# Weighted sums of heads 0 to 7 and 8 to 15 in two banks of PSUM, each half copied by itself

## The chip, the cores and the metric

The kernel runs on one core of a Trainium2 chip. The metric is the time of one execution on the device in microseconds (us). The core has five engines that run their own queues of instructions and wait for one another by semaphores: TensorE (PE in the profile, with its weight loads as PEld), VectorE (DVE), ScalarE (ACT), GpSimd (POOL) and SyncE (SP, which issues DMAs). TensorE writes into PSUM, which has eight banks of 128 x 512 floats; VectorE and ScalarE read it from there.

## The reference

Two transformer blocks in float32 over 16 batches of 128 rows and 128 channels, both with a condition vector per batch. The first has one attention head and an MLP. The second, to which the change belongs, has 16 heads of 8 channels, a padding mask and an MLP:

```python
h = _modulate(_layernorm(x), shift_msa, scale_msa)
qkv = h @ qkv_w.T + qkv_b             # 16 heads of 8 channels
attn = einsum('bhnd,bhmd->bhnm', q, k) * 8 ** -0.5
attn = softmax(where(mask, attn, -1e9))
out = einsum('bhnm,bhmd->bhnd', attn, v)     # the weighted sums
x = x + gate_msa * (out @ proj_w.T + proj_b)
h = _modulate(_layernorm(x), shift_mlp, scale_mlp)
x = x + gate_mlp * (gelu(h @ fc1_w.T + fc1_b) @ fc2_w.T + fc2_b)
```

## The kernel before

Everything stays in the core's memory. Each engine's program is written out by hand, so the order of the instructions in the source is the order on the engine, and `wait_ge` and `then_inc` are all that ties the engines together. The first block works in groups of four batches. The second block's attention works batch by batch in a pipeline: TensorE's `step(b)` (b from 4 to 15; the steps before it are written out one by one) does, in this order,

- `scores(b)`: the scores of batch b, 16 small matrix products in banks 0 to 3 (L340), from which VectorE takes the maxima (`maxima`, L974, two reductions of two banks each);
- `weighted(b - 2)`: the weighted sums of batch b - 2 (L376), 16 products for 16 heads, in groups of four (`j`) that lie side by side in the partitions; `e` is the half of the heads, and `s2` adds the two heads of a slot. Both halves lie in bank 5, in columns 0 to 127 and 128 to 255;
- `back_b(b - 3)`: a transpose of the normalised output (L391);
- `turn_x`: a transpose of the next input (L313), only while b + 7 is below 16, that is up to step 8;
- `back_c(b - 4)`: the projection of an older batch (L396);
- `scores_t(b - 1)`: the scores of batch b - 1 again, transposed, in banks 0, 1, 4 and 5 (L359), from which ScalarE takes the exponentials (`weights_of`, L696, in two halves);
- `back_a(b - 2)`: the transposes of the weighted sums oT (L386), and `turn_maxima(b)` (L365);
- in most steps a projection for the next group (L317, L320, L324) or a piece of the second MLP (L230, L549).

Between `weighted` and `scores_t` stands `back_o`: a copy of the weighted sums out of bank 5 into the tile oT. ScalarE does it for batches 0 to 13 (L707), VectorE for the last two (L1019). `scores_t` of the next batch overwrites banks 4 and 5 and so waits for that copy (`c_oT`). It also waits until the first of VectorE's two reductions has read banks 0 and 1 (`c_max`), and for a DMA that writes the maxima into the queries (`c_nms0`, `c_nms1`). Other copies on ScalarE in a step are onT (L703) and attn (L713), both 128x128 out of bank 7.

Of the kernel before, what the change touches and what calls it, by code (L numbers as in the profile page):

```python
# [10 lines left out]
ACT = mybir.ActivationFunctionType  # L11
AX = mybir.AxisListType

B, N, C = 16, 128, 128
# [27 lines left out]
def build(nc, x, weights, rows, mask, gates, out):  # L42
    with ExitStack() as ctx:
        def sb(name, shape, dt=F32):
            return ctx.enter_context(nc.sbuf_tensor(name, shape, dt))

        def sem(name):
            return ctx.enter_context(nc.semaphore(name))
# [63 lines left out]
        oT = [sb(f"oT{u}", [128, 2, N]) for u in range(2)]  # L112
# [7 lines left out]
        ps = ctx.enter_context(nc.psum_tensor("ps", [128, 8, 512], F32))  # L120
# [5 lines left out]
        def w(name, size=C, at=0):  # L126
            a = W_AT[name] + at
            return W[:, a:a + size]
# [5 lines left out]
        def col(name, j):  # L134
            return w(name, 1, j)
# [13 lines left out]
        s = {n: sem(n) for n in names}  # L149
# [73 lines left out]
        def _(pe):  # L223
            mm = nc.tensor.matmul
# [142 lines left out]
            def weighted(b):  # L367

                pe.wait_ge(s["c_exp"], 2 * b + 2)
                pe.wait_ge(s["c_v"], b // G + 1)  # L370
                v = vx[b // G % 2][:, b % G].rearrange("n (e j s c) -> n e j s c", e=2, j=4, s=2)
                p = pT[b % 2].rearrange("n (e s) j q -> n e j s q", e=2)
                for e in range(2):
                    for s2 in range(2):
                        for j in range(4):
                            ins = mm(ps[32 * j:32 * j + 32, 5, N * e:N * e + N], v[:, e, j, s2], p[:, e, j, s2],  # L376
                                     start=(s2 == 0), stop=(s2 == 1), skip_group_check=True)
                ins.then_inc(s["c_PV"], 1)

            def back_a(b):  # L380
                pe.wait_ge(s["c_oT"], b + 1)
# [16 lines left out]
            def step(b):  # L398

                scores(b)  # L400
                weighted(b - 2)
                back_b(b - 3)
                if b + LEAD < B:
# [34 lines left out]
            for j in range(4):  # L438
                ins = mm(ps[:, 7, B * j:B * j + B], w(("film1", "film2")[j // 2], C, C * (j % 2)), w("cond", B),
                         start=(j == 0), stop=True, skip_group_check=True)  # L440
# [11 lines left out]
            for n, j in enumerate((1, 4, 0, 3)):  # L452
                ins = mm(ps[:, 7, B * n:B * n + B], w("ada", C, C * j), silu[:], start=True, stop=True,
                         skip_group_check=True)
# [7 lines left out]
            for n, j in enumerate((2, 5)):  # L462
                ins = mm(ps[0:B, 6, 2 * C + C * n:3 * C + C * n], silu[:], w("ada", C, C * j), start=True, stop=True,
                         skip_group_check=True)
# [60 lines left out]
            turn_maxima(1)  # L525
            scores(2)
            weighted(0)
            pe.wait_ge(s["c_nm"], 2)
            turn_x(LEAD + 1)
# [6 lines left out]
            project_k(1)  # L536
            scores(3)
            weighted(1)
            back_b(0)
            pe.wait_ge(s["c_k"], 2)  # L540
# [63 lines left out]
        def _(act):  # L604
            a = nc.scalar.activation
# [97 lines left out]
                a(onT[b % 2][:], ps[:, 7, 2 * N:3 * N], ACT.Copy).then_inc(s["c_onT"], 1)  # L703

            def back_o(b):
                act.wait_ge(s["c_PV"], b + 1)
                a(oT[b % 2][:], ps[:, 5, 0:2 * N].rearrange("p (e n) -> p e n", e=2), ACT.Copy).then_inc(s["c_oT"], 1)  # L707

            def projected(b):
                act.wait_ge(s["c_pr"], b + 1)  # L710
# [4 lines left out]
            def step(b):  # L715
                if 0 <= b - 2:
                    weights_of(b - 2, 1)
                if b == 3 or b > 3 and b % G == 2 and b // G + 1 < B // G:
                    front_k(b // G + 1)
                elif b == 4 or b > 4 and b % G == 3 and b // G + 1 < B // G:  # L720
                    front_v(b // G + (1 if b > 4 else 0))
                if b in (B - 4, B - 1):
                    affine("d_", (b - (B - 4)) // 3, 3, bank(6), (0, 1, 2))
                if b in (B - 3, B - 2):
                    raw(b - (B - 3))
                if 0 <= b - 2 < B:
                    back_o(b - 2)
                if 0 <= b - 3:
                    turned_o(b - 3)
                if 0 <= b - 4:  # L730
                    projected(b - 4)
                if b == 2:
                    front_h(LEAD + 1)
                if b > 1 and b + LEAD < B:
                    front_h(b + LEAD)
                if b in (B - 4, B - 1):
                    affine("d_", (b - (B - 4)) // 3, 3, bank(6), (3,))
                if 0 <= b - 1 < B:
                    weights_of(b - 1, 0)
# [44 lines left out]
        def _(dve):  # L784
            v = nc.vector
# [67 lines left out]
            for b in (2, 3):  # L853
                ins = v.tensor_scalar(xn[0][:, b], xs[:, b], rstd[:, 0, b:b + 1], None, ALU.mult)
# [43 lines left out]
            for n, j in enumerate((1, 4, 0, 3)):  # L898

                dst = scale[:, 2 + n, :] if n < 2 else shift[:, n, :]  # L900
                ins = v.tensor_scalar(dst, ps[:, 7, B * n:B * n + B], col("cols1", COL1["ada"] + j),
                                      1.0 if n < 2 else 0.0, ALU.add, ALU.add)
# [112 lines left out]
                v.tensor_copy(onT[b % 2][:], ps[:, 7, 2 * N:3 * N]).then_inc(s["c_onT"], 1)  # L1015

            def back_o(b):
                dve.wait_ge(s["c_PV"], b + 1)
                v.tensor_copy(oT[b % 2][:], ps[:, 5, 0:2 * N].rearrange("p (e n) -> p e n", e=2)).then_inc(s["c_oT"], 1)  # L1019

            def projected(b):
                dve.wait_ge(s["c_pr"], b + 1)
# [20 lines left out]
            for b in range(2, B):  # L1043
                step(b)
                if b == 2:
                    statistics(2, 3)
            next_statistics(B - 5)
            back_o(B - 2)
            normalise(B - 2)
            next_statistics(B - 4)  # L1050
            d_norm(2)
            turned_o(B - 2)
            back_o(B - 1)
            projected(B - 2)
            normalise(B - 1)
# [205 lines left out]
```

## Time and profile before

| | |
|---|---|
| median of 3 runs | 185.45 us (184.04 to 185.47) |
| the profiled execution | 185.37 us, of which its span 183.5 us |
| TensorE's granted clock | 1.00 of full speed over the whole span |
| busy: TensorE, its weight loads | 175.1 us (95%), 135.1 us (74%) |
| busy: VectorE, ScalarE, GpSimd | 122.0 us (66%), 110.7 us (60%), 100.7 us (55%) |

The span runs from the first to the last instruction of the profiled execution. The steps of the second block's attention lie between 76 and 152 us; one step takes some 5.2 us. A row of the timeline gives the start, the duration, the engine, the line, the operation and the tiles that it writes and reads; "x32" are 32 instructions in a row, and what stands in brackets is the engine's idle time before them and who ended it. The products of this kernel are in float32, and each shows as two instructions in TensorE's rows. Ends of matrix products are modelled, so a load (PEld) says better than a product when TensorE could go on.

### The profile page before, as it was taken

The page shows a single profiled execution, that of the slowest core. Times are in us where ns is not written, and L with a number is a line of the kernel's source. Part 1 is how long each engine was busy: PE and PEld are TensorE (multiplying, and loading weights), DVE is VectorE, ACT ScalarE, POOL GpSimd, SP SyncE. Part 2 cuts the span into 40 slices and gives each one's busy share as a digit, 9 for nine tenths or more (in the row PEclk, how much of TensorE's full clock was granted, in tenths as well). Part 3 has the DMA queues.
Part 4 walks back from the last instruction along what each step waited for, and adds up shares of the span by engine and source line. Part 5 has one row for each costly group of instructions (what it writes and reads, how often), then busy time and mean ns, then how long its engine had stood idle before and what let it go on. Part 6 is the DMA issues. An engine that isn't in the chain of part 4 may idle for free.

```text
span 183.5 us, 5666 instructions
## 1 busy us (share of the span) xinstructions
PE 175.1 (95%) x2250; PEld 135.1 (74%) x2250; DVE 122.0 (66%) x372; ACT 110.7 (60%) x229; POOL 100.7 (55%) x187
## 2 busy tenths in 40 slices
PE   6999999899999999999999989999999999999994
PEld 6986777678476698878768866787677755768593
DVE  6789869859315269585776777887788855562334
ACT  6425876793982830577656665676755877956500
POOL 8929999969850205934546642975087466470000
PEclk9999999999999999999999999999999999999999
DMA  4992000211900300101011001010000000001103
GB/s 112 401 413 112 4 0 14 63 24 43 389 25 0 120 0 5 59 5 59 4 62 63 5 2 62 7 63 4 5 5 5 2 5 0 4 0 57 61 0 114
DMA packets 4277, 10.91 MB, mean 59 GB/s; under 512 B 540, under 2 KB 1260, under 8 KB 3948
## 3 DMA queue, kind: packets, MB, share of 16 engines
q1 hardware_dynamic: 3788, 8.83, 13.5%
q10 hardware_dynamic: 464, 1.73, 2.5%
q8 instruction: 18, 0.29, 0.7%
q14 instruction: 7, 0.06, 0.1%
HBM read 7.24 MB, written 1.09 MB: 45 GB/s over the span
## 4 chain that ended last, share of the span: by engine, by line
PE 82%; POOL 11%; ACT 2%; issue 2%; DVE 1%; POOLq 0%; DVEq 0%
PE ps L305 16%; PE ps L292 13%; PE ps L359 10%; PE ps L340 10%; PE ps L376 9%; PE ps L433 4%; POOL xn L1105 3%; POOL xb L1091 3%; PE ps L386 3%; POOL rstd L1086 2%; PE ps L230 2%; PE ps L317 2%; PE ps L324 2%; PE ps L396 2%; PE ps L391 2%; PE ps L320 2%
## 5 line engine op out<-in xcount | busy, mean ns | idle before, releaser
L974 DVE TENSOR_REDUCE nm<-ps 128x8 f32<-128x1024 f32 x32 | 37.7, 1219 | 8.7 <-PE ps L340 8.7
L696 ACT ACTIVATE shared<-ps 128x1024 f32<-128x1024 f32 x32 | 31.0, 1021 | 16.5 <-PE ps L359 16.5
L1086 POOL TENSOR_TENSOR rstd<-var_eps,half 128x4 f32<-128x4 f32 x16 | 16.3, 1020 | 37.3 <-DVE var_eps L818 19.3
L305 PEld LDWEIGHTS ps<-W,hid 128*128 128x128 f32 x256 | 29.6, 192 | 1.7 <-issue 1.4
L305 PE MATMUL ps<-W,hid 128*128 128x128 f32 x256 | 30.3, 276 | 0.0
L292 PE MATMUL ps<-hT,W 128*128 128x512 f32 x56 | 25.9, 596 | 0.0
L663 ACT ACTIVATE hid<-ps,W 128x512 f32<-128x512 f32 x28 | 18.2, 693 | 6.7 <-PE ps L292 6.7
L340 PEld LDWEIGHTS ps<-k_pad,q_pad 32*128 32x128 f32 x512 | 15.8, 186 | 8.3 <-issue 7.8
L622 ACT ACTIVATE hT<-ps,shift,scale 128x128 f32<-128x128 f32 x44 | 16.9, 466 | 7.8 <-PE ps L230 7.8
L359 PE MATMUL ps<-q_pad,k_pad 32*128 32x128 f32 x512 | 18.8, 282 | 1.5 <-ACT oT L707 0.5
L340 PE MATMUL ps<-k_pad,q_pad 32*128 32x128 f32 x512 | 18.8, 283 | 1.4 <-ACT shared L696 1.4
L359 PEld LDWEIGHTS ps<-q_pad,k_pad 32*128 32x128 f32 x512 | 16.2, 186 | 4.1 <-issue 4.0
L1174 POOL TENSOR_TENSOR gated<-attn,gate 128x128 f32<-128x128 f32 x16 | 7.3, 457 | 19.5 <-ACT attn L713 15.7
L376 PE MATMUL ps<-shared,vx 128*32 128x128 f32 x512 | 17.3, 276 | 0.0
L292 PEld LDWEIGHTS ps<-hT,W 128*128 128x128 f32 x56 | 9.9, 191 | 9.4 <-issue 8.4
L376 PEld LDWEIGHTS ps<-shared,vx 128*32 128x32 f32 x512 | 13.0, 109 | 2.3 <-issue 0.5
L707 ACT ACTIVATE oT<-ps 128x256 f32<-128x256 f32 x14 | 5.4, 384 | 15.4 <-PE ps L376 15.4
L980 DVE COPY nmT<-ps 16x128 f32<-16x128 f32 x16 | 4.4, 278 | 13.0 <-PE ps L365 12.9
L1105 POOL TENSOR_SCALAR xn<-xs,rstd 128x128 f32<-128x128 f32 x30 | 10.8, 378 | 0.8
L797 DVE BATCH_NORM_STATS2 bn<-xs 128x6 f32<-128x128 f32 x48 | 10.4, 280 | 0.3 <-DMA xs<-x 0.2
L947 DVE TENSOR_TENSOR gmul<-ps,gate 128x512 f32<-128x512 f32 (+2 forms) x6 | 3.1, 512 | 10.2 <-PE ps L305 10.2
L433 PE MATMUL ps<-ident 128*128 128x128 f32 x32 | 7.5, 430 | 1.5 <-POOL ident L1074 1.5
(132 smaller groups left out, 324.9 us busy)
## 6 DMA issues: line engine op xcount, KB each, us to landing
gate<-gates SPq DMA_DIRECT2D x1, 2048.0 KB, 7.0
xs<-x SPq DMA_DIRECT2D x4, 256.0 KB, 5.7
gate<-mask ACTq DMA_DIRECT2D x1, 1024.0 KB, 10.3
q_pad<-apT SPq DMA_DIRECT2D x4, 256.0 KB, 2.4
k_pad<-apT SPq DMA_DIRECT2D x4, 256.0 KB, 2.4
W<-weights SPq DMA_DIRECT2D x1, 768.0 KB, 11.7
out<-xs SPq DMA_DIRECT2D x3, 256.0 KB, 2.3
W<-weights SPq DMA_DIRECT2D x1, 512.0 KB, 8.0
```

Of the source, the lines that this page charges most:

```text
L292: mm(ps[:, h_bank + f, :], w(w1, C, C * f), hT[g % 2][:], start=True, stop=True).then_inc(s[p + "M1"], 1)
L305: ins = mm(bank(o_bank)[:, j], hid[g % 2][:, f, j], w(w2, C, C * f), start=(f == 0), stop=(f == FC - 1), skip_group_check=True)
L340: ins = mm(bank(r)[:, t], q_pad[some, t, b], k_pad[some, t, b], start=True, stop=True, skip_group_check=True)
L359: ins = mm(bank((0, 1, 4, 5)[r])[:, t], k_pad[some, t, b], q_pad[some, t, b], start=True, stop=True, skip_group_check=True)
L376: ins = mm(ps[32 * j:32 * j + 32, 5, N * e:N * e + N], v[:, e, j, s2], p[:, e, j, s2], start=(s2 == 0), stop=(s2 == 1), skip_group_check=True)
L433: mm(ps[:, 3, 0:C], ident[:], ident[:], start=True, stop=True)
L622: ins = a(hT[g % 2][:, j], src[:, j], ACT.Identity, bias=shift[:, k, b:b + 1], scale=scale[:, k, b:b + 1])
L663: a(hid[g % 2][:, f], bank(h_bank + f), func, bias=col(bcols, bat + f)).then_inc(s[p + "gelu"], 1)
L696: a(pT[b % 2][:, 2 * e:2 * e + 2], ps[:, 4 * e:4 * e + 2, :].rearrange("n r (t q) -> n r t q", t=4), ACT.Exp, scale=HD ** -0.5).then_inc(s ...
L974: v.tensor_reduce(nm[b % 2][:, 8 * e:8 * e + 8], ps[:, 2 * e:2 * e + 2, :].rearrange("n r (t k) -> n (r t) k", t=4), AX.X, ALU.max, negate ...
L1086: p.tensor_tensor(rstd[:, k, G * g:G * g + G], var_eps[:, k, G * g:G * g + G], half[:, 0:G], ALU.pow)\
L1105: ins = p.tensor_scalar(xn[g % 2][:, j], xs[:, b], rstd[:, k, b:b + 1], 0.0, ALU.mult, ALU.add)
```

## The change

The sums of heads 0 to 7 go to bank 4 and those of heads 8 to 15 to bank 5, both in columns 0 to 127. TensorE signals after each half, so `c_PV` counts two for a batch. `back_o`, on both engines that have it, copies each half when it is signalled, with one signal `c_oT` after the second.

```diff
@@ TensorE, weighted(b)
                 for e in range(2):
                     for s2 in range(2):
                         for j in range(4):
-                            ins = mm(ps[32 * j:32 * j + 32, 5, N * e:N * e + N], v[:, e, j, s2], p[:, e, j, s2],
+                            ins = mm(ps[32 * j:32 * j + 32, 4 + e, 0:N], v[:, e, j, s2], p[:, e, j, s2],
                                      start=(s2 == 0), stop=(s2 == 1), skip_group_check=True)
-                ins.then_inc(s["c_PV"], 1)
+                    ins.then_inc(s["c_PV"], 1)
@@ ScalarE
             def back_o(b):
-                act.wait_ge(s["c_PV"], b + 1)
-                a(oT[b % 2][:], ps[:, 5, 0:2 * N].rearrange("p (e n) -> p e n", e=2), ACT.Copy).then_inc(s["c_oT"], 1)
+                for e in range(2):
+                    act.wait_ge(s["c_PV"], 2 * b + e + 1)
+                    ins = a(oT[b % 2][:, e], ps[:, 4 + e, 0:N], ACT.Copy)
+                ins.then_inc(s["c_oT"], 1)
@@ VectorE
             def back_o(b):
-                dve.wait_ge(s["c_PV"], b + 1)
-                v.tensor_copy(oT[b % 2][:], ps[:, 5, 0:2 * N].rearrange("p (e n) -> p e n", e=2)).then_inc(s["c_oT"], 1)
+                for e in range(2):
+                    dve.wait_ge(s["c_PV"], 2 * b + e + 1)
+                    ins = v.tensor_copy(oT[b % 2][:, e], ps[:, 4 + e, 0:N])
+                ins.then_inc(s["c_oT"], 1)
```

On ScalarE, in step 6 of the attention (`shared` is where the exponentials go, `apT` the keys of the next group, `hc` the next input, modulated), there stands before:

```order
L696 ACTIVATE shared<-ps 128x1024 [waits c_T] x2
L683 ACTIVATE apT<-ps,W 128x512 [waits c_ks,c_K]
L707 ACTIVATE oT<-ps 128x256 [waits c_PV]
L703 ACTIVATE onT<-ps 128x128 [waits c_pr,c_T3]
L713 ACTIVATE attn<-ps 128x128 [waits c_ga,c_pr]
L676 ACTIVATE hc<-ps,shift,scale 128x128 [waits ada_ok,c_Tx]
```

And on ScalarE in the same place of the changed kernel:

```order
L696 ACTIVATE shared<-ps 128x1024 [waits c_T] x2
L683 ACTIVATE apT<-ps,W 128x512 [waits c_ks,c_K]
L708 ACTIVATE oT<-ps 128x128 [waits c_PV] x2
L703 ACTIVATE onT<-ps 128x128 [waits c_pr,c_T3]
L715 ACTIVATE attn<-ps 128x128 [waits c_ga,c_pr]
L676 ACTIVATE hc<-ps,shift,scale 128x128 [waits ada_ok,c_Tx]
```

One copy of 128x256 has become two of 128x128, each with a wait of its own, and nothing else has moved. TensorE's instructions stand in the same order in both kernels; in a step with `turn_x` they are, from the weighted sums to the transposes of oT:

```order
L376 MATMUL ps<-shared,vx 32x128 [waits c_v,c_exp]
L376 MATMUL ps<-shared,vx 32x128 x15
L391 MATMUL ps<-ident,on 128x128 [waits c_on]
L313 MATMUL ps<-ident,xc 128x128 [waits c_xc,c_v]
L396 MATMUL ps<-W,onT 128x128 [waits c_nm,c_onT]
L359 MATMUL ps<-q_pad,k_pad 128x128 [waits c_oT,c_max,c_nms1]
L359 MATMUL ps<-q_pad,k_pad 128x128 x15
L386 MATMUL ps<-ident,oT 128x128 [waits c_onT,c_at,c_oT]
```

What has moved there is only the bank that the first half of L376 writes, and the signal after it.

## Rows read from the trace of the kernel before

**Rows 1.** The page's chain that ended last: share of the span by engine.

```profile
PE 82%; POOL 11%; ACT 2%; issue 2%; DVE 1%; POOLq 0%; DVEq 0%
```

**Rows 2.** The chain in order of time (start us, us, what), steps 3 and 11.

```profile
82.83 0.39 ACT oT L707
83.22 0.14 issue
...
123.57 1.01 PE ps L376 x32
124.58 0.26 PE ps L391
124.84 0.22 PE ps L396 x2
125.07 0.11 issue
125.18 1.21 PE ps L359 x32
```

**Rows 3.** Timeline, step 11 (no `turn_x`).

```profile
121.31 0.97 PEld L324 LDWEIGHTS ps<-W,hc 128*128 128x128 f32 x8
122.40 0.98 PEld L340 LDWEIGHTS ps<-k_pad,q_pad 32*128 32x128 f32 x32
123.50 0.81 PEld L376 LDWEIGHTS ps<-shared,vx 128*32 128x32 f32 x32
123.64 2.36 DVE L974 TENSOR_REDUCE nm<-ps 128x8 f32<-128x1024 f32 x2 [0.59 <-PE ps L340]
124.51 0.14 PEld L391 LDWEIGHTS ps<-ident,on 128*128 128x128 f32 x1 [0.20 <-issue]
124.52 0.36 PEld L396 LDWEIGHTS ps<-W,onT 128*128 128x128 f32 x2
124.65 0.38 ACT L707 ACTIVATE oT<-ps 128x256 f32<-128x256 f32 x1 [1.00 <-PE ps L376]
125.15 1.01 PEld L359 LDWEIGHTS ps<-q_pad,k_pad 32*128 32x128 f32 x32 [0.27 <-issue]
```

**Rows 4.** Timeline, step 8 (with `turn_x`).

```profile
108.95 0.38 ACT L707 ACTIVATE oT<-ps 128x256 f32<-128x256 f32 x1 [1.48 <-PE ps L376]
108.98 0.30 PEld L396 LDWEIGHTS ps<-W,onT 128*128 128x128 f32 x2
109.45 1.01 PEld L359 LDWEIGHTS ps<-q_pad,k_pad 32*128 32x128 f32 x32 [0.17 <-issue]
```

**Rows 5.** Timeline, step 9.

```profile
113.37 2.35 DVE L974 TENSOR_REDUCE nm<-ps 128x8 f32<-128x1024 f32 x2
114.68 1.01 PEld L359 LDWEIGHTS ps<-q_pad,k_pad 32*128 32x128 f32 x32 [0.28 <-issue]
```

**Rows 6.** Lines by themselves: duration in ns (min/median/max), first and last start in us.

```profile
L707 ACT ACTIVATE oT<-ps x14: 384/384/385, 77.6 to 145.4; 128x256 f32<-128x256 f32 x14
L703 ACT ACTIVATE onT<-ps x14: 271/278/278, 83.1 to 149.9; 128x128 f32<-128x128 f32 x14
L1019 DVE COPY oT<-ps x2: 425/425/425, 150.8 to 156.8; 128x256 f32<-128x256 f32 x2
L1015 DVE COPY onT<-ps x2: 280/286/292, 155.8 to 159.2; 128x128 f32<-128x128 f32 x2
L974 DVE TENSOR_REDUCE nm<-ps x32: 1212/1215/1225, 64.5 to 145.6; 128x8 f32<-128x1024 f32 x32
```

**Rows 7.** Waits in total (us, times, longest); timeline of step 12 and the end.

```profile
PEld ps L359 <- issue: 4.0, 15, 0.4
...
128.24 1.16 ACT L622 ACTIVATE hT<-ps,shift,scale 128x128 f32<-128x128 f32 x3
129.83 0.38 ACT L707 ACTIVATE oT<-ps 128x256 f32<-128x256 f32 x1 [0.43 <-PE ps L376]
...
150.76 0.42 DVE L1019 COPY oT<-ps 128x256 f32<-128x256 f32 x1 [0.99 <-PE ps L376]
151.30 1.01 PEld L359 LDWEIGHTS ps<-q_pad,k_pad 32*128 32x128 f32 x32 [0.38 <-issue]
...
157.56 0.20 PEld L386 LDWEIGHTS ps<-ident,oT 128*128 128x128 f32 x2 [0.20 <-issue]
```

## Prediction

> **What bounds the kernel now.** I read the page's chain first, because it says which engine's work sets the end: TensorE holds 82% of it [rows 1]. So an edit pays only where it lets TensorE start earlier, and ScalarE's or VectorE's own busy time counts for nothing by itself. Then I read the same chain in order of time over one batch of the second block [rows 2]. The reader is to see that TensorE's pieces follow one another without a hole, except one: after the weighted sums (L376), the transpose of the normalised output (L391) and the projection (L396), there stand 0.11 us of "issue" before the transposed scores (L359). The profile names no one for that hole. The timeline of the same step does [rows 3]: ScalarE's copy oT (L707) runs from 124.65 to 125.03, and the first weight load of L359 is at 125.15, 0.12 later. At step 3 the chain goes through the copy itself: 82.83 to 83.22, then 0.14 of issue [rows 2]. I find the same 0.11 to 0.12 us between the copy's end and the next L359 load in all 14 steps with a ScalarE copy and at the one VectorE copy before L359 (150.76 + 0.42 = 151.18, load at 151.30) [rows 6, 7]. The copy is therefore the last thing that the transposed scores wait for, 15 times, although the table of waits lists this idle time as "issue", 4.0 us of TensorE's weight loader in 15 places [rows 7].
>
> **What the change does, part by part.**
>
> *The copy in two halves.* Before, one copy of 128x256 starts when the last of the weighted sums is there. Now heads 0 to 7 land in bank 4, heads 8 to 15 in bank 5, and each half is copied when its own sums are there. After the last sum only a copy of 128x128 is left. The old copy takes 384 ns; ScalarE's copy of 128x128 from PSUM (onT, L703) takes 278: 0.384 - 0.278 = 0.106 us less per step. On VectorE 0.425 - 0.286 = 0.139 (L1019 against L1015) [rows 6].
>
> *Does the first half get out of the way?* The 32 loads of L376 take 0.81 us, so the first half's are done 0.40 before the second's, and its copy can start at about 124.65 - 0.40 = 124.25 and end at 124.53, before 124.65 [rows 3]. ScalarE is free then in that step. In the tightest step that I found it is busy until 129.40 and idle for 0.43 before the copy at 129.83 [rows 7]: the first half runs to about 129.7 and still doesn't hold the second. The first half's wait is on a signal that comes before the old one, so what is queued behind it (onT, attn, the next exponentials) waits for nothing longer. The additional instruction costs nothing on the path while this cover of 0.12 us holds; without it, it would cost up to a whole copy of 0.278.
>
> *The additional signal on TensorE.* The trace shows no signal in the middle of L376, so I bound it. L391 signals, and the load of L396 follows it without a gap (124.51 + 0.14, against 124.52): cost 0. From above: the loader stands for 0.20 us behind the signalling end of L376 before L391 loads [rows 3]; were all of that the signal, it would be 0.20 per step. I take 0, since L391 is the plainer case and the 0.20 comes with a change of the tile's shape. A gain is excluded, because nothing is removed from TensorE.
>
> *A rule against this.* The row shows no gap behind a signalling matmul [rows 3]. The Trainium skill, TensorE: Matmul & The Clock Gate, section "The cost: per-tile semaphore tail", says that increments of a packed group are serialised and that each lengthens its tail by about 26 ns. By that rule the 15 steps would give back an estimated 0.4 us, and the sum would be 0.8 instead of 1.24. No run here shows such a tail.
>
> *What is late next.* Three things can hold L359 once the copy is shorter.
> - The first half of the maxima (L974), which must have read banks 0 and 1. In step 11 it ends at 123.64 + 1.215 = 124.86, the old copy at 125.03, the new one at 124.93: the copy is still last, by 0.07 [rows 3, 6]. In step 9 VectorE starts late, at 113.37, so its half ends at 114.58 and the load is at 114.68: the maxima bind as well, and the gain there is 0, at most 0.106 [rows 5].
> - TensorE's own work. From one load of 128 rows to the next of 32 rows the loader needs 0.12 us where nobody is waited for (L324 ends at 122.28, L340 loads at 122.40) [rows 3]. In step 11 L396's loads end at 124.88, so the floor is 125.00; the copy's release falls from 125.15 to 125.05, and the whole 0.106 counts. In steps 4 to 8 there is another transpose ahead of L396 (L313): L396's loads end at 109.28 and L359 loads at 109.45, a gap of 0.17 [rows 4]. Above the floor of 0.12 there are 0.05 us to be had, five times.
> - The exponentials and the next scores follow the transposed scores, so they move with them and give nothing back.
>
> *The second copy on VectorE* (156.81) is followed by other transposes; the loader stands for 0.20 before L386 at 157.56, as long as before L391, and the copy ends at 156.81 + 0.425 = 157.24 [rows 3, 7]. No gain there, at most 0.139.
>
> *The sum.* Steps 2 and 3: 2 x 0.106 = 0.21. Steps 4 to 8: 5 x 0.05 = 0.25 (0 to 0.53). Step 9: 0 (0 to 0.11). Steps 10 to 15: 6 x 0.106 = 0.64. The VectorE copy before the last L359: 0.14. Together 1.24 us, with ends of 0.99 and 1.63 (1.77 with the last VectorE copy). The profiled execution took 185.37 us, of which 183.5 is its span; the 1.87 around it don't change. 185.37 - 1.24 = 184.13. The median of the runs shown lies 0.08 above the profiled execution: **184.2 us**, 0.7% faster. A difference under 1% is about what a measurement of this kernel can't tell from no change: its three runs lie 1.4 us apart.
>
> **The rivals.**
> - *The whole copy time comes off everywhere* (the floor of 0.12 is not one, and the maxima don't bind in step 9). For it: in steps 4 to 8, too, the load comes 0.12 behind the copy (109.33 to 109.45). Against it: the chain there runs through TensorE alone. 14 x 0.106 and 0.14 give 1.62, with the last VectorE copy 1.76: 183.7 to 183.8. It passes 1% only with a fast reading on top.
> - *Something else is hardly earlier than the copy.* The 0.07 us by which the maxima are earlier are worked out with a release as quick as the copy's. If VectorE's release takes 0.1 longer, the maxima bind in steps 10 to 15 as in step 9, and what is left is steps 2 to 8 and the end, 0.21 + 0.25 + 0.14 = 0.60: 184.9. Against it: in step 9 VectorE's half ends at 114.58 and the load is 0.10 behind, no slower than ScalarE.
> - *The signal in the middle stops TensorE* as long as the end of L376 seems to: place, between the heads' halves; price 15 x 0.20 = 3.0 us, all on the chain; 3.0 - 1.24 = 1.8 slower, 187.2. It turns the sign from 0.08 per step on; a smaller price leaves part of the gain, and is counted with the forecast. Against it: no gap behind L391, which signals as well.
> - *The change does nothing for time,* since the first half's copy is held up on ScalarE and the second stands behind it. The cover is 0.12 us, and if it fails everywhere, second halves end where the old copy ended: 185.4.
>
> **How the numbers follow.** Forecast 0.58; whole copy time 0.18; maxima next 0.11; nothing 0.06; signal stops TensorE 0.07. The first reaches from 183.8 to 184.6, with the runs' scatter. Faster by over 1% (under 183.6) takes the whole copy time and a fast reading: 0.17. Slower by over 1% (over 187.3) is the signal at its full price, or a slow reading: 0.05. Within 1%: 0.78. The range takes in the whole copy time and the nothing case with its scatter: 183.2 to 185.6; it leaves out the signal and the extremes of the scatter.
>
> **What would show it.** In the changed kernel's timeline: two oT copies of about 0.28 us per step, the first about 0.40 ahead of the second; L359's load about 0.38 to 0.40 behind the second's start in steps 10 to 15, against 0.50 now; 0.16 to 0.17 idle before it in steps 4 to 8 shrunk to about 0.12; L376 with 0.81 us of loads as before. The forecast is wrong if L376's loads have a hole in the middle, if the second copy starts later behind its sums than 124.65 does now, if L359 is held by VectorE in more steps than 9, or if a step's period shrinks by more than 0.106.

## The result, and the profile after

The changed kernel takes **182.96 us** (median of 11 runs, 182.58 to 184.12), the kernel before in the same comparison 184.15 us (11 runs, 183.96 to 185.47). The ratio is 0.9935, with a 95% interval of 0.9913 to 0.9958: 1.2 us or 0.65% faster (0.8 to 1.6 us). The forecast was 1.24 us less, but a time of 184.2 with a range from 183.2: the difference was met, the time lies below the range. The reason is the time that the difference was taken from, and four of the nine experiments (5, 6, 8 and 9) are about it.

The profiled execution of the changed kernel took 183.18 us (span 181.4). Its timeline in step 11, to be read beside [rows 3] (L708 is the copy of a half, L976 the maxima):

```profile
121.98 0.81 PEld L376 LDWEIGHTS ps<-shared,vx 128*32 128x32 f32 x32
122.09 2.36 DVE L976 TENSOR_REDUCE nm<-ps 128x8 f32<-128x1024 f32 x2 [0.59 <-PE ps L340]
122.69 0.28 ACT L708 ACTIVATE oT<-ps 128x128 f32<-128x128 f32 x1 [0.59 <-PE ps L376]
122.99 0.14 PEld L391 LDWEIGHTS ps<-ident,on 128*128 128x128 f32 x1 [0.20 <-issue]
123.00 0.36 PEld L396 LDWEIGHTS ps<-W,onT 128*128 128x128 f32 x2
123.13 0.28 ACT L708 ACTIVATE oT<-ps 128x128 f32<-128x128 f32 x1 [0.16 <-PE ps L376]
123.52 1.01 PEld L359 LDWEIGHTS ps<-q_pad,k_pad 32*128 32x128 f32 x32 [0.17 <-issue]
```

The first half's copy starts 0.44 ahead of the second's and is done in time. The second starts 1.15 behind the first load of L376, exactly as the one copy did before (123.50 to 124.65), and ends at 123.41; L359 loads 0.11 later. L359's load now stands 1.54 behind L376's first, before 1.65. The copies by themselves (duration in ns, min/median/max; first and last start):

```profile
L708 ACT ACTIVATE oT<-ps x28: 277/277/278, 76.3 to 143.5; 128x128 f32<-128x128 f32 x28
L1022 DVE COPY oT<-ps x4: 291/292/293, 148.3 to 154.6; 128x128 f32<-128x128 f32 x4
```

And the table of waits, against 4.0 us in 15 places [rows 7]:

```profile
PEld ps L359 <- issue: 2.2, 10, 0.3
```

In step 8 (with `turn_x`) and step 9, beside [rows 4, 5]:

```profile
107.60 0.28 ACT L708 ACTIVATE oT<-ps 128x128 f32<-128x128 f32 x1 [0.16 <-PE ps L376]
107.63 0.30 PEld L396 LDWEIGHTS ps<-W,onT 128*128 128x128 f32 x2
108.06 0.98 PEld L359 LDWEIGHTS ps<-q_pad,k_pad 32*128 32x128 f32 x32
...
111.94 2.35 DVE L976 TENSOR_REDUCE nm<-ps 128x8 f32<-128x1024 f32 x2
112.75 0.28 ACT L708 ACTIVATE oT<-ps 128x128 f32<-128x128 f32 x1 [0.16 <-PE ps L376]
113.23 1.01 PEld L359 LDWEIGHTS ps<-q_pad,k_pad 32*128 32x128 f32 x32 [0.25 <-issue]
```

In step 8 L359 no longer follows the copy (end 107.88, load 0.18 later) but L396, 0.13 behind its last load. Its 32 loads take 0.98 us there, before 1.01 [rows 4]; so it is in each of steps 4 to 8, where L359 no longer waits for a copy, and the step behind each of them gains these 0.03 as well. In step 9 L359 follows the maxima: the first half ends at 111.94 + 1.215 = 113.16, the load comes 0.07 later, while the copy was done at 113.03. The DMA that writes the maxima into the queries had landed 1.50 us ahead of that load, by the trace's times of its semaphore, so it is not what holds L359 there.

To see only the attention I measure a **stretch**: from the first load of L359 of batch 0 to that of batch 15. Before, it runs from 72.16 to 151.30: 79.14 us. After, from 71.30 to 149.11: 77.81. The change has taken 1.33 us out of the attention, and by steps (how much earlier L359's first load stands, against the step ahead of it): steps 2 and 3: 0.11, 0.10; steps 4 to 8: 0.04, 0.08, 0.07, 0.08, 0.05; step 9: 0.06; steps 10 to 15: 0.10, 0.08, 0.11, 0.10, 0.11, 0.11; the last L359, behind VectorE's copy: 0.13. But 0.86 us lie ahead of the attention, where the change touches nothing.

### The profile page after: what moved, and what is told of

Read it like the earlier page. It is cut to its first block, busy times and chain, and to the rows that moved or that the text cites. A ratio compares the mean times of both kernels' runs of the same rounds, so it can differ in the third digit from the quotient of the medians.

```text
span 181.4 us, 5682 instructions
## 1 busy us (share of the span) xinstructions
PE 173.0 (95%) x2250; PEld 133.1 (73%) x2250; DVE 122.4 (67%) x374; ACT 113.1 (62%) x243; POOL 100.3 (55%) x187
## 4 chain that ended last, share of the span: by engine, by line
PE 81%; POOL 11%; DVE 4%; ACT 2%; issue 2%; POOLq 0%; DVEq 0%
PE ps L305 16%; PE ps L292 13%; PE ps L359 10%; PE ps L340 9%; PE ps L376 8%; POOL xn L1109 3%; POOL xb L1095 3%; PE ps L386 3%; PE ps L433 3%; POOL rstd L1090 2%; PE ps L230 2%; PE ps L396 2%; PE ps L317 2%; PE ps L324 2%; PE ps L391 2%; PE ps L320 2%
## 5 line engine op out<-in xcount | busy, mean ns | idle before, releaser
L976 DVE TENSOR_REDUCE nm<-ps 128x8 f32<-128x1024 f32 x32 | 37.7, 1218 | 8.7 <-PE ps L340 8.7
L359 PE MATMUL ps<-q_pad,k_pad 32*128 32x128 f32 x512 | 18.8, 282 | 0.5
L359 PEld LDWEIGHTS ps<-q_pad,k_pad 32*128 32x128 f32 x512 | 16.0, 186 | 2.9 <-issue 2.2
L376 PE MATMUL ps<-shared,vx 128*32 128x128 f32 x512 | 17.3, 276 | 0.0
L708 ACT ACTIVATE oT<-ps 128x128 f32<-128x128 f32 x28 | 7.8, 277 | 11.5 <-PE ps L376 11.5
L376 PEld LDWEIGHTS ps<-shared,vx 128*32 128x32 f32 x512 | 13.0, 109 | 2.3 <-issue 0.5
L949 DVE TENSOR_TENSOR gmul<-ps,gate 128x512 f32<-128x512 f32 (+2 forms) x6 | 3.1, 511 | 10.2 <-PE ps L305 10.2
L230 PE MATMUL ps<-ident,xn 128*128 128x128 f32 x48 | 7.3, 275 | 2.0 <-POOL xn L1109 1.1
## 6 DMA issues: line engine op xcount, KB each, us to landing
gate<-mask ACTq DMA_DIRECT2D x1, 1024.0 KB, 10.2
```

The costliest lines, as they stand in the source:

```text
L230: ins = nc.tensor.transpose(dst[:, j], src[:, j], ident[:])
L359: ins = mm(bank((0, 1, 4, 5)[r])[:, t], k_pad[some, t, b], q_pad[some, t, b], start=True, stop=True, skip_group_check=True)
L376: ins = mm(ps[32 * j:32 * j + 32, 4 + e, 0:N], v[:, e, j, s2], p[:, e, j, s2], start=(s2 == 0), stop=(s2 == 1), skip_group_check=True)
L976: v.tensor_reduce(nm[b % 2][:, 8 * e:8 * e + 8], ps[:, 2 * e:2 * e + 2, :].rearrange("n r (t k) -> n (r t) k", t=4), AX.X, ALU.max, negate ...
```

## The experiments

Every kernel's time stands against the kernel before on the same chip.

**1. Two banks, one copy.** What is left of the change is the second bank.

```diff
-                    ins.then_inc(s["c_PV"], 1)
+                ins.then_inc(s["c_PV"], 1)
...
-                for e in range(2):
-                    act.wait_ge(s["c_PV"], 2 * b + e + 1)
-                    ins = a(oT[b % 2][:, e], ps[:, 4 + e, 0:N], ACT.Copy)
-                ins.then_inc(s["c_oT"], 1)
+                act.wait_ge(s["c_PV"], b + 1)
+                a(oT[b % 2][:], ps[:, 4:6, 0:N], ACT.Copy).then_inc(s["c_oT"], 1)
```

(the same on VectorE)

> The sums in two banks, but one signal and one copy of 128x256 out of both, as long as the copy of the kernel before (0.384 us). Measured by the stretch from the first load of L359 (step 1) to the last (end), which is 79.14 us in the kernel before and 77.81 in the changed one. Theory (the gain is the shorter last copy): 79.1, time as before. Rival (the second bank itself, or the other form of the read, brings the gain): 77.8, time 0.65% under before.

Measured: ratio 0.9992 (0.9968 to 1.0016); stretch 71.49 to 150.64, 79.15. The copy takes its old time again, and L359 its old place behind it:

```profile
L707 ACT ACTIVATE oT<-ps x14: 384/384/384, 76.9 to 144.8; 128x256 f32<-128x256 f32 x14
```

The second bank alone brings nothing.

**2. Both halves late.** The changed kernel, with the first half's wait put back to the second signal.

```diff
-                    act.wait_ge(s["c_PV"], 2 * b + e + 1)
+                    act.wait_ge(s["c_PV"], 2 * b + 2)
```

(the same on VectorE)

> Two banks, two signals and two copies as in the changed kernel, but the first half's copy waits for the second signal too. Theory: the second copy starts 0.18 us behind the first (as attn behind onT) and ends 0.18 + 0.277 = 0.46 behind the last sum, 0.07 later than the single copy of before: 15 x 0.07 = 1.1 more, a stretch of 80.2, time 0.6% over before. Rival (smaller copies are enough, the early start of the first is not needed): under 79.1.

Measured: ratio 1.0043 (1.0019 to 1.0068), stretch 71.29 to 151.37, 80.08. Step 11:

```profile
124.21 0.36 PEld L396 LDWEIGHTS ps<-W,onT 128*128 128x128 f32 x2
124.35 0.45 ACT L708 ACTIVATE oT<-ps 128x128 f32<-128x128 f32 x2 [1.02 <-PE ps L376]
124.91 1.01 PEld L359 LDWEIGHTS ps<-q_pad,k_pad 32*128 32x128 f32 x32 [0.34 <-issue]
```

Two copies one behind the other take 0.45 where one takes 0.384, and 0.94 us come on top of the stretch, in 15 steps 0.06 each. Without the early start the split costs; the copy's end is what L359 waits for, in this direction too.

**3. A signal on each product.** Sixteen signals in L376 in place of two.

```diff
-                    ins.then_inc(s["c_PV"], 1)
+                            ins.then_inc(s["c_PV"], 1)
...
-                    act.wait_ge(s["c_PV"], 2 * b + e + 1)
+                    act.wait_ge(s["c_PV"], 16 * b + 8 * e + 8)
```

(the same on VectorE)

> The changed kernel with a signal on each of the 16 products of the weighted sums, 14 more per batch. Theory (a signal costs TensorE nothing): stretch 77.8, time as the changed kernel. Rival by the increments' tail of 26 ns each: 14 x 0.026 = 0.36 per batch, in 15 steps on the path 5.5 us: 83.3. Rival by the 0.20 us that the loader stands behind L376 (all of it the signal): 14 x 0.20 x 15 = 42 us more.

Measured: ratio 0.9966 (0.9938 to 0.9993), stretch 72.32 to 151.03, 78.71: 0.9 more than the changed kernel, neither 0 nor 5.5 nor 42. Step 11:

```profile
123.44 0.81 PEld L376 LDWEIGHTS ps<-shared,vx 128*32 128x32 f32 x32
124.23 0.28 ACT L708 ACTIVATE oT<-ps 128x128 f32<-128x128 f32 x1 [0.68 <-PE ps L376]
124.67 0.28 ACT L708 ACTIVATE oT<-ps 128x128 f32<-128x128 f32 x1 [0.16 <-PE ps L376]
125.06 1.01 PEld L359 LDWEIGHTS ps<-q_pad,k_pad 32*128 32x128 f32 x32 [0.24 <-issue]
```

TensorE's loads take the same 0.81 us, so nothing stops. But the second copy starts 1.23 behind the first load instead of 1.15: the last signal arrives 0.08 us later. Fourteen more signals cost 0.08, the one in the middle of the changed kernel nothing that the rows show (1.15 before and after). So the first theory holds for one signal that lies 0.4 us ahead of the last, and falls for signals that lie close together. The first half's copy, which waits for the eighth signal, is late by the same 0.08 (0.79 behind the first load, in the changed kernel 122.69 - 121.98 = 0.71): the delay doesn't grow from the eighth signal to the sixteenth. The Trainium skill, TensorE: Matmul & The Clock Gate, section "The cost: per-tile semaphore tail", gives 26 ns for each; by it 14 would be an estimated 0.36 us, and the trace shows less than a quarter of it. That only the last few signals stand in line would fit, but wasn't tried.

**4. A last copy of 16 columns.** What would be next if the copy were shorter still.

```diff
-                for e in range(2):
-                    act.wait_ge(s["c_PV"], 2 * b + e + 1)
-                    ins = a(oT[b % 2][:, e], ps[:, 4 + e, 0:N], ACT.Copy)
-                ins.then_inc(s["c_oT"], 1)
+                act.wait_ge(s["c_PV"], 2 * b + 1)
+                a(oT[b % 2][:, 0], ps[:, 4, 0:N], ACT.Copy)
+                a(oT[b % 2][:, 1, 16:N], ps[:, 4, 16:N], ACT.Copy)
+                act.wait_ge(s["c_PV"], 2 * b + 2)
+                a(oT[b % 2][:, 1, 0:16], ps[:, 5, 0:16], ACT.Copy).then_inc(s["c_oT"], 1)
```

> On ScalarE the copy behind the last sum takes only 16 columns of the second half; the other 112 columns of the second half of oT are filled from the first half's bank, so the output of heads 8 to 15 is left out for those rows. The last copy should take about 0.185 us in place of 0.277. Theory (TensorE's own floor of 0.12 and the maxima are next): no gain in steps 2, 4 to 8 and 9, 0.06 in step 3, 0.04 to 0.05 in steps 10 to 15, together 0.33: stretch 77.5. Rival (the copy is all that L359 waits for): 14 x 0.092 = 1.3, stretch 76.5.

Measured: ratio 0.9910 (0.9875 to 0.9946), stretch 70.94 to 148.30, 77.36, that is 0.45 less than the changed kernel. By steps: 0.04 and 0.10 in steps 2 and 3, 0 in steps 4 to 9 together (the load of step 3 stands 0.50 earlier than in the changed kernel, that of step 9 too), 0.05, 0.07, 0.07, 0.08, -0.04 and 0.05 in steps 10 to 15, 0.03 at the end. Steps 8, 11 and 14 (L977 are the maxima):

```profile
107.10 0.18 ACT L710 ACTIVATE oT<-ps 128x16 f32<-128x16 f32 x1
107.14 0.30 PEld L396 LDWEIGHTS ps<-W,onT 128*128 128x128 f32 x2
107.56 0.98 PEld L359 LDWEIGHTS ps<-q_pad,k_pad 32*128 32x128 f32 x32
...
122.42 0.36 PEld L396 LDWEIGHTS ps<-W,onT 128*128 128x128 f32 x2
122.55 0.18 ACT L710 ACTIVATE oT<-ps 128x16 f32<-128x16 f32 x1
122.90 0.98 PEld L359 LDWEIGHTS ps<-q_pad,k_pad 32*128 32x128 f32 x32
...
136.80 2.35 DVE L977 TENSOR_REDUCE nm<-ps 128x8 f32<-128x1024 f32 x2
138.09 1.01 PEld L359 LDWEIGHTS ps<-q_pad,k_pad 32*128 32x128 f32 x32 [0.23 <-issue]
```

In steps 8 and 11 L359 loads 0.12 behind L396's last load, whatever the copy does: in step 11 the copy ended 0.17 ahead. This is TensorE's floor as forecast; the rival of 1.3 us is out. In step 14 L359 follows VectorE's first half, which ends at 136.80 + 1.215 = 138.02, by the same 0.07 as in step 9 of the changed kernel; that is the step that loses 0.04. The gain is over the 0.33 of the theory because it left out the 0.03 by which L359 is shorter when it doesn't wait (0.98 in step 11, in the changed kernel 1.01). A last copy that is 0.09 shorter would thus still give some 0.45.

**5. The time that the difference was taken from.** The times of the kernel before come in two groups: of its 84 runs in this study 60 lie from 183.84 to 184.76 (median 184.15) and 24 from 185.20 to 185.54 (median 185.42). Two of the three runs ahead of the prediction, and the profiled execution, were of the upper group. The two profiles differ ahead of the attention: in the second spin (L433), products on the identity that nobody uses. Before (the loads of the second spin, and the first of L359):

```profile
7.43 2.68 PEld L433 LDWEIGHTS ps<-ident 128*128 128x128 f32 x12
72.16 0.98 PEld L359 LDWEIGHTS ps<-q_pad,k_pad 32*128 32x128 f32 x32
```

After:

```profile
7.06 1.42 PEld L433 LDWEIGHTS ps<-ident 128*128 128x128 f32 x12
71.30 0.98 PEld L359 LDWEIGHTS ps<-q_pad,k_pad 32*128 32x128 f32 x32
```

A load takes 0.223 in one and 0.118 in the other, about double: TensorE runs at the lower of its two levels (1.2 GHz) in one and at the higher (2.4 GHz) in the other, although the column of the granted clock says 1.00 in both, and the transfers run alike (windows from 6.0 to 10.2 us; PE, PEld, DVE, ACT and POOL with their instructions, then the clock, the DMA share and GB/s). Before:

```profile
6.00:10.20 4.20, 4.20 (x21) 4.20 (x21) 3.23 (x22) 1.94 (x2) 2.96 (x5) 1.00 1.05 411
```

After:

```profile
6.00:10.20 4.20, 3.25 (x27) 3.09 (x27) 3.60 (x22) 1.87 (x2) 2.93 (x5) 1.00 1.05 409
```

The trace's record of the granted clock begins, with 1.00, at 10.60 us in the profile of the kernel before and at 6.62 in that of the changed one, and holds nothing ahead of that; the 1.00 "over the whole span" in the table of the time before is therefore true only from 10.60 us on. The loads tell the same: in the changed kernel they start every 0.21 us up to 6.6 and every 0.11 from there.

TensorE had done the same in both until the end of the first spin: 20 loads of the first spin in 4.34 us, at the lower level. I took the first spin away from the kernel before:

```diff
-            spin(10)
```

> The kernel before without the ten products on the identity with which TensorE starts (their results are never used). Theory (the upper of the two groups of times, 185.3 to 185.5 against 184.0 to 184.7, are executions in which TensorE is still at the lower of its two clock levels in its second spin, L433): with less work ahead of it TensorE is at the lower level there in every execution, the second spin's 12 loads take 2.7 us, and all times are at 185.3 or above. Rival (the groups come from the transfers or from the launch): nothing but unused work is gone, and the lowest times stay at 184.0.

Measured: 185.73 to 186.25 in six runs, ratio 1.0088 (1.0058 to 1.0117); no run of the lower group is left. The second spin's loads take 2.68 us. The stretch is 79.57: in the profiled execution the loads of L359 in step 8 take 1.44 us in place of 1.01, with a hole among them that no other profile has and that I can't explain; it is not part of the theory.

**6. The kernel before again.** No edit.

> The kernel before, unchanged, for a second profile. Theory of the groups: if its profiled time is at 184.0 to 184.7, the second spin's 12 loads take 1.4 us and the first load of L359 stands at 71.3 to 71.5; if it is at 185.3 or above, 2.7 us and 72.2. In both the stretch between the first and the last load of L359 is 79.1. Rival: the profile of a lower time shows the second spin at 2.7 us as well, and the stretch is what differs.

Measured: profiled time 184.76, the highest of the lower group and 0.06 over the expected one; stretch 71.54 to 150.70, 79.16.

```profile
7.24 1.42 PEld L433 LDWEIGHTS ps<-ident 128*128 128x128 f32 x12
71.54 0.98 PEld L359 LDWEIGHTS ps<-q_pad,k_pad 32*128 32x128 f32 x32
150.70 1.01 PEld L359 LDWEIGHTS ps<-q_pad,k_pad 32*128 32x128 f32 x32 [0.38 <-issue]
```

The same kernel, 0.61 faster than in the first profile, and all of it (72.16 - 71.54 = 0.62) lies ahead of the attention. That is half of the 1.27 between the medians of the two groups; the lower group is 0.9 wide, and this execution is at its upper end.

**7. ScalarE's halves alone.** VectorE copies its two batches whole, as before.

```diff
-                for e in range(2):
-                    dve.wait_ge(s["c_PV"], 2 * b + e + 1)
-                    ins = v.tensor_copy(oT[b % 2][:, e], ps[:, 4 + e, 0:N])
-                ins.then_inc(s["c_oT"], 1)
+                dve.wait_ge(s["c_PV"], 2 * b + 2)
+                v.tensor_copy(oT[b % 2][:], ps[:, 4:6, 0:N]).then_inc(s["c_oT"], 1)
```

> The changed kernel, but VectorE copies both halves of its two batches at once behind the second signal (the last two batches), as before the change. Theory: the last step loses its 0.13: stretch 77.94. Rival (the end isn't bound by that copy): 77.81.

Measured (one run): stretch 72.10 to 150.00, 77.90. The last step, from the load of step 15 to the last L359, takes 5.35 us as before the change; in two profiles of the changed kernel it takes 5.22. VectorE's part is 0.13.

**8. The changed kernel again.** No edit.

> The changed kernel again, beside more runs of the kernel before on one chip. Theory: ratio 0.9935, that is 1.2 to 1.3 us under before within each group of times; stretch 77.8.

Measured: 182.93 (9 runs, 182.55 to 184.15), ratio 0.9929 (0.9898 to 0.9959); profiled time 183.86, stretch 72.03 to 149.79, 77.76.

```profile
7.43 2.68 PEld L433 LDWEIGHTS ps<-ident 128*128 128x128 f32 x12
72.03 0.98 PEld L359 LDWEIGHTS ps<-q_pad,k_pad 32*128 32x128 f32 x32
149.79 1.01 PEld L359 LDWEIGHTS ps<-q_pad,k_pad 32*128 32x128 f32 x32 [0.25 <-issue]
```

This profile is of the changed kernel's upper group (in its 20 runs 14 lie from 182.55 to 183.18, median 182.75, and 6 from 183.86 to 184.15, median 183.96), and its second spin takes 2.68 like that of the first profile of the kernel before. Like against like: 183.86 against 185.37, and 183.18 against 184.76, 1.5 and 1.6 us less, and 1.4 and 1.5 by the medians of the groups; 1.3 to 1.4 of it are the stretch, and the remainder is what lies ahead of the attention, which varies by 0.6 within a group too (table below).

**9. The changed kernel with an earlier spin.** TensorE's first spin runs on a tile that VectorE clears first.

```diff
+            v.memset(hT[0][:, 0], 0.0).then_inc(s["warm_ok"], 1)
             v.memset(half[:], -0.5).then_inc(s["half_ok"], 1)
...
-            pe.wait_ge(s["ident_ok"], 2)
-            spin(10)
+            pe.wait_ge(s["warm_ok"], 1)
+            for _ in range(11):
+                mm(ps[:, 3, 0:C], hT[0][:, 0], hT[0][:, 0], start=True, stop=True)
+            pe.wait_ge(s["ident_ok"], 2)
```

> The changed kernel, with TensorE's first spin (11 unused products) on a tile that VectorE clears as its first instruction, so that TensorE need not wait for the identity and starts about 0.4 us earlier (at 1.1 in place of 1.51). Theory (what separates the two groups is when TensorE comes to its higher clock level): the level rises earlier too, the median comes 0.1 to 0.4 under the changed kernel's 182.95, the stretch stays at 77.8, and the lower group's share doesn't fall. Rival (the start doesn't depend on when TensorE starts): 182.95, lowest 182.55.

Measured: 182.72 (7 runs, 182.65 to 183.13), ratio to the kernel before 0.9908 (0.9873 to 0.9943); stretch 71.18 to 148.95, 77.77.

```profile
1.04 4.76 PEld L437 LDWEIGHTS ps<-hT 128*128 128x128 f32 x22 [1.04 <-DVE hT L790]
...
7.03 1.42 PEld L433 LDWEIGHTS ps<-ident 128*128 128x128 f32 x12
```

TensorE starts at 1.04 instead of 1.51, with one product more. Its clock's record begins at 6.42 us, inside the 5.10 to 7.02 of kernels that start at 1.51 (table below), so that the level rises earlier isn't shown. None of the seven runs is of the upper group, where 6 of 20 of the changed kernel are; by chance alone that would happen about once in 12 times (0.7 to the seventh power), so it is a hint. The median is 0.2 under the changed kernel's, inside both intervals. It is the lowest median of a kernel with a complete output here, but that it beats the changed kernel isn't shown.

All profiles together, in order of the time that is left when the stretch is taken off (the last column is when the trace's record of the granted clock begins; three traces have none):

| kernel | profiled time | second spin | stretch | rest | clock record from |
|---|---|---|---|---|---|
| 16 columns (4) | 182.38 | 1.42 | 77.36 | 105.02 | 5.10 |
| early spin (9) | 182.99 | 1.42 | 77.77 | 105.22 | 6.42 |
| both late (2) | 185.42 | 1.42 | 80.08 | 105.34 | 6.24 |
| changed | 183.18 | 1.42 | 77.81 | 105.37 | 6.62 |
| one copy (1) | 184.71 | 1.42 | 79.15 | 105.56 | 6.91 |
| before again (6) | 184.76 | 1.42 | 79.16 | 105.60 | 7.02 |
| changed again (8) | 183.86 | 2.68 | 77.76 | 106.10 | none |
| ScalarE alone (7) | 184.07 | 2.68 | 77.90 | 106.17 | none |
| no first spin (5) | 185.77 | 2.68 | 79.57 | 106.20 | none |
| before | 185.37 | 2.68 | 79.14 | 106.23 | 10.60 |
| a signal each (3) | 185.11 | 2.68 | 78.71 | 106.40 | 10.96 |

The rest falls into two groups, and the second spin says which. Inside the first it grows with the time at which the record begins, from 105.02 at 5.10 us to 105.60 at 7.02, with one pair out of order. So the lower group is not one value either: within it, too, a later rise goes with a longer time. The stretch goes with the kernel: two profiles of the kernel before differ in it by 0.02, two of the changed kernel by 0.05; only the hole in experiment 5 stands out.

## Why the prediction was wrong, and where it was right

**The step that failed** is the last of the sum, the base: "The median of the runs shown lies 0.08 above the profiled execution". Median and profiled execution both stood for executions in which TensorE comes late to its higher level, and these are 24 of the 84 on record. With a base of 185.45 in place of the 184.15 that eleven runs give, 1.3 us too much went into the time and into both ends of the range. That two of three runs fell into the smaller group was bad luck, which at that share (two or three of three) comes about one time in five; that the base rested on them was the error. The text even gave the runs' distance of 1.4 us, and read it as scatter around one value. It was two values, 184.04 and twice 185.45 or so, and the loads of L433 in the profile, 0.223 us each beside 0.15 or less for loads of the same shape later, showed that TensorE was still at its lower level in the second spin; that other executions are not was to be seen only in a second profile. From a base of 184.15 the forecast would have been 184.15 - 1.24 = 182.9.

**The copy in two halves**: right. 0.277 measured for 0.278, 0.292 for 0.286. That the shorter last copy is the cause is shown from three sides: without the early start the gain turns into a loss of 0.94 in the stretch (2), with one copy it is 0 (1), and a still shorter copy brings more, but no more than until TensorE's floor or the maxima (4).

**The cover of the first copy**: right; it started 0.44 ahead of the second, and the second waits for its sums.

**The signal in the middle**: taken at 0, and 0 in the rows. As a general rule the argument (no gap behind L391) was too short: sixteen signals delay the last by 0.08 (3). The rival in which a signal stops TensorE for 0.20 is out, since the loads of L376 take 0.81 us with sixteen signals too.

**What is late next**: right in kind, with a term missing. In steps 4 to 8 TensorE's floor binds, with 0.04 to 0.08 for the forecast 0.05; the sum is 0.32 for 0.25. The floor itself gives 0.04 to 0.05, and the remainder is L359 itself, whose loads take 0.98 us in place of 1.01 when it doesn't wait. In step 9 the gain was 0.06, not 0. The reading that "the maxima bind as well" there was wrong: before, the load stood 0.11 behind the copy's end (114.18 + 0.385 = 114.57) as in every other step, and 0.10 behind VectorE's half only because of that; where VectorE's half is last, the load follows it by 0.07 (after, and in experiment 4). That gives 0.02 to 0.03, and 0.03 come from the shorter L359 of step 8. Steps 10 to 15 gave 0.61 for 0.64, steps 2 and 3 0.21 as forecast, the end 0.13 for 0.14. The second copy on VectorE has no gain to show.

**The sum**: 1.24 forecast, 1.33 to 1.40 in the stretch, 0.8 to 1.6 us by the ratio's interval. Faster by 0.65% is within 1%, which had 0.78.

**Still open**: what decides in an execution when TensorE comes to its higher level; with the same first spin from 1.51 us on, the record begins anywhere from 5.10 to 7.02, or at 10.60 and 10.96. That it depends on TensorE's work at the start is shown (5); whether an earlier start secures the early rise is not (9).

## What to carry to other kernels

A copy that stands between two stages costs from the last input to its own end, so copying early what is ready early pays the difference between a long and a short copy, once per step, and no more than until the next thing that binds; list these floors step by step, and the gain can be told closely (here 1.24 for 1.33 to 1.40 us). Splitting alone costs: two copies in a row are longer than one. And before a forecast is made against a time, look whether the runs form groups, and into which the profiled execution falls: a difference of 0.7% was forecast well here and lost in a base that was 0.7% off.

## What the runs showed of the hardware that was not expected

- In 24 of 84 executions of the kernel before, by their times, TensorE is at its lower level some 4 us longer at the start (in the profiles: 12 loads of the second spin in 2.68 us instead of 1.42, the clock's record from 10.6 us or later instead of 5.1 to 7.0). It costs 0.63 us in the two profiles of the kernel before and 0.73 in those of the changed one (column "rest"), 1.2 to 1.3 between the medians of the groups, and the profile's granted clock reads 1.00 all the while.
- Sixteen signals within 0.8 us of TensorE's work delay the last one by 0.08 us, and the eighth by as much, without slowing the loads (experiment 3); two that lie 0.4 apart don't delay each other.
- L359's 32 loads take 0.98 us when TensorE goes on to them without a wait, and 1.01 when it waited (steps 8 and 11 after, step 8 before).
- TensorE's loader takes 0.12 to 0.13 us from the last load of L396 to the first of L359 whether the copy ended 0.17 or 0.28 ahead of that load (experiment 4, steps 11 and 8).
